# Softmax scores of two graph layers taken by streaming the edges past a one-column weight tile

## The reference

```python
# layer 1 ("attention")
z = feature @ W_out + b_out
e = gelu(z[src] @ attn_w[:d] + z[dst] @ attn_w[d:])
a = exp(e - segment_max(e, dst)[dst]); a = a / segment_sum(a, dst)[dst]
h = segment_sum(a[:, None] * z[src], dst) + feature @ res_W + res_b
# layer 2 ("relations")
att = sum(proj[src, etype] * tanh(proj[dst, etype] + efeat), axis=-1)
a = exp(att - segment_max(att, dst)[dst]); a = a / segment_sum(a, dst)[dst]
h_nb = segment_sum(nfeat[src] * a[:, None], dst)
```

## Time and profile before

| | |
|---|---|
| three runs | 4811.55, 4816.27, 4816.76 us; median 4816.27 |
| the profiled execution | 4814.14 us, of which 4812.4 us from its first to its last instruction (the span) |
| busy shares of the span | PE 85%, PEld 61%, DVE 67%, POOL 58%, ACT 41% |
| attention phase | from 1994 to about 2574 us |
| relation phase | from about 2577 to about 3775 us |
| granted clock of TensorE | 0.877 of full speed over the span; two levels occur, 2.4 GHz (1.00) and 1.2 GHz (0.50) |

### The profile page before, as it was taken

How to read it: one execution, slowest core, us unless ns; L and a number is a source line. 1 busy time by engine, 2 the same in 40 slices (tenths; PEclk the granted TensorE clock), 3 DMA queues, 4 the chain that set the end, 5 groups by cost and what they waited for, 6 DMA issues and landing times. The chain is left out here.

```text
span 4812.4 us, 78524 instructions
## 1 busy us (share of the span) xinstructions
PE 4094.3 (85%) x23907; PEld 2928.3 (61%) x24119; DVE 3210.3 (67%) x7115; ACT 1960.9 (41%) x3684; POOL 2811.1 (58%) x2859
## 2 busy tenths in 40 slices
PE   5989999799989999779986899898988677767776
PEld 1278888688877777578884455555555344444443
DVE  9967777666667888667776588888887433333332
ACT  0066666344445454224332155555555222222221
POOL 0066665667656666577753455554551377777777
PEclk9989999899989999755556899999998798899888
DMA  1089998799976676445543444444442222222221
GB/s 40 1 260 287 288 287 264 197 230 235 234 200 174 192 194 191 122 111 127 127 113 84 97 103 109 105 112 103 114 105 56 66 66 67 54 67 67 55 65 29
DMA packets 1127654, 649.03 MB, mean 135 GB/s; under 512 B 908912, under 2 KB 944313, under 8 KB 1127240
## 3 DMA queue, kind: packets, MB, share of 16 engines
q1 hardware_dynamic: 1039432, 555.85, 42.2%
q0 software_dynamic: 87808, 88.16, 9.2%
HBM read 384.70 MB, written 261.63 MB: 134 GB/s over the span
## 5 line engine op out<-in xcount | busy, mean ns | idle before, releaser
L2237 POOL DMA_INDIRECT r_got<-x_table,slot_idx x392 | 417.6, 1065 | 588.9 <-DVE r_masked L2470 280.7
L1089 POOL DMA_INDIRECT o_rows<-in_x_dram,dst_idx x392 | 370.7, 946 | 443.6 <-POOLq L348 241.7
L2552 POOL DMA_INDIRECT m_rows<-x_table,slot_idx x392 | 376.3, 960 | 223.6 <-issue 118.6
L2336 PE MATMUL r_source_t<-r_masked,rel_pair 64*128 64x512 f32 x980 | 501.3, 660 | 0.0
L2338 PE MATMUL r_own_t<-r_masked,rel_pair 64*128 64x512 f32 x980 | 501.2, 660 | 0.0
L2691 DVE TENSOR_TENSOR_SCAN m_both<-m_keep,m_both,m_rows_t 128x512 f32<-128x512 bf16 x97 | 124.1, 1279 | 553.1 <-PE m_rows_t L2614 553.1
L1541 POOL DMA_INDIRECT b_rows<-h_table,slot_idx x392 | 369.7, 943 | 206.9 <-issue 91.5
L1352 POOL DMA_INDIRECT a_got<-node_table,src_idx x392 | 375.5, 958 | 194.8 <-DVE a_conv L1488 57.3
L2560 POOL DMA_INDIRECT out_dram<-s_res,put_out x392 | 390.6, 996 | 137.8 <-issue 109.7
L2010 POOL DMA_INDIRECT t_got<-x_table,slot_idx x392 | 379.0, 967 | 144.8 <-issue 95.4
L2336 PEld LDWEIGHTS r_source_t<-r_masked,rel_pair 64*128 64x128 f32 x980 | 197.4, 211 | 239.0 <-issue 189.9
(11 more groups left out here) (401 smaller groups left out, 11670.1 us busy)
## 6 DMA issues: line engine op xcount, KB each, us to landing
x_table<-n_res SPq DMA_DIRECT2D x196, 256.0 KB
n_rows<-x_table SPq DMA_DIRECT2D x196, 256.0 KB
x_table<-s_res SPq DMA_DIRECT2D x294, 128.0 KB
node_table<-n_wide SPq DMA_DIRECT2D x98, 272.0 KB, 3.9
h_table<-n_conv SPq DMA_DIRECT2D x98, 256.0 KB
x_table<-s_res SPq DMA_DIRECT2D x98, 256.0 KB
r_feats<-in_edge_attr_dram SPq DMA_DIRECT2D x390, 64.0 KB
n_rows<-in_x_dram SPq DMA_DIRECT2D x97, 256.0 KB
```

The source lines that it names most:

```text
L1089: nc.gpsimd.indirect_dma_start(out=rows[:, n % 4, t, :], out_offset=None, in_=x, in_offset=bass.IndirectOffsetOnAxis(ap=dst_idx[:, n * TIL ...
L2237: nc.gpsimd.indirect_dma_start(out=got[:, n % RING, t, :], out_offset=None, in_=x2_table, in_offset=bass.IndirectOffsetOnAxis(ap=slot_idx[ ...
L2336: nc.tensor.matmul(source_t[:, :], rel_pair[0:D, k, :], masked[0:D, n % 2, k, :], start=(k == 0), stop=(k == PAIRS - 1), skip_group_check= ...
L2552: nc.gpsimd.indirect_dma_start(out=rows[:, n % 4, t, 0:D], out_offset=None, in_=x3_table, in_offset=bass.IndirectOffsetOnAxis(ap=slot_idx[ ...
```

## The change

`match` swaps the two operands. The weights are now a 128x128 tile that is zero but for one column: a window into a tile of 255 columns whose column 127 holds `score_col` (or ones). The window's offset puts this column at the tile's place in the chunk (0 to 27), and 128 edges are streamed past it. All 28 tiles of a chunk are summed into one 128x128 PSUM bank, whose first 28 rows then hold the chunk's scores in the softmax's layout; the other rows get zeros. In the attention phase one more matmul at a chunk's end adds the source part (`source_score` as weights against the identity), for which PE waits for DVE's `score_kept`. `add_scores` (DVE) and `turn_scores` (PE) are gone, ACT writes `score` into SBUF at once, and the wait for `shares_kept` moves from `turn_scores` to `turn_ends`. Each phase gets one or two more small instructions on DVE at its start that make the 255-column tile.

```diff
-            self.score_t = [pb(c, f"f_score_t{h}", [P, rows]) for h in range(score_banks)]
+            self.score_t = [pb(c, f"f_score_t{h}", [P, P]) for h in range(score_banks)]
-            self.score = self.small_t[0:rows, 384:384 + P]
-            self.kept_score = sb(c, "f_kept_score", [P, 2, rows])
+            self.score = sb(c, "f_score", [rows, P])
...
+        def slide(self, columns, n, t):
+            at = P - 1 - (self.row_of(n) * TILES + t)
+            return columns[:, at:at + P]
...
+        def keep(self, act, c, func, bias=None):
+            act.wait_ge(self.scored[c], self.scored.done(c))
+            if c >= 1:
+                act.wait_ge(self.belows[c - 1], self.belows.done(c - 1))
+            of = self.score_t[c % len(self.score_t)][0:self.rows, :]
...
+                nc.scalar.activation(self.score[:, :], of, func, bias=bias).then_inc(self.kept[c], 1)
...
-        def turn_scores(self, pe, c):
-            pe.wait_ge(self.kept[c], self.kept.done(c))
-            if c >= 1:
-                pe.wait_ge(self.shares_kept[c - 1], self.shares_kept.done(c - 1))
-            nc.tensor.transpose(self.score, self.kept_score[:, c % 2, :], ident[:, :]).then_inc(self.scores_turned[c], 1)
...
         def raise_rows(self, dve, c):
-            dve.wait_ge(self.scores_turned[c], self.scores_turned.done(c))
+            dve.wait_ge(self.kept[c], self.kept.done(c))
...
         def turn_ends(self, pe, c):
-                pe.wait_ge(self.total_entered[c - 1], self.total_entered.done(c - 1))
+                pe.wait_ge(self.shares_kept[c - 1], self.shares_kept.done(c - 1))
...
@@ attention_phase
                     def match(n):
                         pe.wait_ge(scanned[n], scanned.done(n))
-                        if n // CHUNK >= 2:
-                            pe.wait_ge(score_added[n // CHUNK - 2], score_added.done(n // CHUNK - 2))
+                        if n == 0:
+                            pe.wait_ge(cleared, 4)
+                        if n % CHUNK == 0 and n // CHUNK >= 2:
+                            pe.wait_ge(soft.kept[n // CHUNK - 2], soft.kept.done(n // CHUNK - 2))
                         for t in range(TILES):
-                            last = nc.tensor.matmul(soft.score_at(n, t), scan[:, n % SCANS, t * P:(t + 1) * P], score_col[:, :],
-                                                    start=True, stop=True, skip_group_check=True)
+                            nc.tensor.matmul(soft.bank_of(n)[:, :], soft.slide(score_cols, n, t), scan[:, n % SCANS, t * P:(t + 1) * P],
+                                             start=(n % CHUNK == 0 and t == 0), stop=False, skip_group_check=True)
                         if n % CHUNK == CHUNK - 1:
-                            last.then_inc(soft.scored[n // CHUNK], 1)
+                            k = n // CHUNK
+                            pe.wait_ge(score_kept[n], score_kept.done(n))
+                            nc.tensor.matmul(soft.bank_of(n)[0:soft.rows, :], source_score[:, k % 2].rearrange("p j t -> p (j t)"), ident[:, :],
+                                             start=False, stop=True, skip_group_check=True).then_inc(soft.scored[k], 1)
...
+                    nc.vector.memset(score_cols[:, :], 0.0).then_inc(cleared, 1)
+                    dve.wait_ge(cleared, 3)
+                    nc.vector.tensor_copy(score_cols[:, P - 1:P], score_col[:, :]).then_inc(cleared, 1)
...
@@ relation_phase
                         for t in range(TILES):
-                            last = nc.tensor.matmul(soft.score_at(n, t), pair[:, n % 2, t * P:(t + 1) * P], ones[:, 0:1],
-                                                    start=True, stop=True, skip_group_check=True)
+                            last = nc.tensor.matmul(soft.bank_of(n)[:, :], soft.slide(ones_cols, n, t), pair[:, n % 2, t * P:(t + 1) * P],
+                                                    start=(n % CH == 0 and t == 0), stop=(n % CH == CH - 1 and t == TILES - 1),
+                                                    skip_group_check=True)
...
+                    nc.vector.memset(ones_cols[:, :], 0.0).then_inc(cleared, 1)
+                    dve.wait_ge(cleared, 3)
+                    nc.vector.memset(ones_cols[:, P - 1:P], 1.0).then_inc(cleared, 1)
                     nc.vector.memset(scan[0:D, :, :], 0.0).then_inc(tops_cleared, 1)
```

More of the change, by code:

```diff
@@ L1765, in columns_of, with bank_of @@
             return slice(self.row_of(n) * TILES, self.row_of(n) * TILES + TILES)
[L1767 to L1772, removed]
+        def bank_of(self, n):
+            return self.score_t[n // self.chunk % len(self.score_t)]
+        def slide(self, columns, n, t):
+            at = P - 1 - (self.row_of(n) * TILES + t)
+            return columns[:, at:at + P]
         def load_first(self, sp):
@@ L1809, in raise_rows @@
                 dve.wait_ge(self.gaps[c - 1], self.gaps.done(c - 1))
-            nc.vector.tensor_tensor_scan(self.run(self.values()), self.run(self.low[:, c % 2, :]), self.run(self.score), LOW,
+            nc.vector.tensor_tensor_scan(self.run(self.values()), self.run(self.low[:, c % 2, :]), self.run(self.score[:, :]), LOW,
                                          ALU.add, ALU.max).then_inc(self.raised[c], 1)
@@ L1845, in raise_all @@
             dve.wait_ge(self.entered[c], self.entered.done(c))
-            nc.vector.tensor_tensor_scan(self.run(self.values()), self.run(self.low[:, c % 2, :]), self.run(self.score),
+            nc.vector.tensor_tensor_scan(self.run(self.values()), self.run(self.low[:, c % 2, :]), self.run(self.score[:, :]),
                                          self.entry(), ALU.add, ALU.max).then_inc(self.peaked[c], 1)
@@ L1852, in soften @@
                 dve.wait_ge(self.weighed[c - 1], self.weighed.done(c - 1))
-            nc.vector.tensor_tensor(self.below[:, :], self.score, self.values(), ALU.subtract).then_inc(self.belows[c], 1)
+            nc.vector.tensor_tensor(self.below[:, :], self.score[:, :], self.values(), ALU.subtract).then_inc(self.belows[c], 1)
             if c >= 1:
@@ L2088, in keep_chunk @@
                     def keep_chunk(eng, k):
-                        soft.keep(eng, k, ACT.Gelu, whole_score[:, k % 2, :], score_added, score_bias[:, 0:1])
+                        soft.keep(eng, k, ACT.Gelu, score_bias[0:soft.rows, 0:1])
                     def lift(b):
@@ L2154, in keep_shares @@
                         soft.keep_shares(eng, k, weighed, (k - 1) * CHUNK - 1)
[L2156 to L2161, removed]
-                                                source_score[:, k % 2].rearrange("p j t -> p (j t)"), ALU.add).then_inc(score_added[k], 1)
                     def invert(n):
@@ L2173, in _ @@
                                (scale, X + 3, BLOCKS), (powers, X + 2, BLOCKS), (keep_score, 1, BLOCKS),
-                               soft.after(2, add_scores, dve), soft.after(4, soft.raise_rows, dve), soft.after(5, soft.run_peaks, dve),
+                               soft.after(4, soft.raise_rows, dve), soft.after(5, soft.run_peaks, dve),
                                soft.after(6, soft.enter_peaks, dve), soft.after(6, soft.raise_all, dve), soft.after(6, soft.soften, dve),
@@ L2379, in _ @@
                                soft.after(6, soft.turn_ends, pe), soft.after(8, soft.turn_sums, pe), soft.after(9, turn_shares, pe),
[L2380 removed]
+                               soft.after(6, soft.turn_peaks, pe), soft.after(8, soft.turn_totals, pe),
                                (project, 2, BLOCKS))
@@ L2424, in keep_chunk @@
                     def keep_chunk(eng, k):
-                        soft.keep(eng, k, ACT.Copy, soft.scores_of(k), soft.scored)
+                        soft.keep(eng, k, ACT.Copy)
                     over_turns(soft.after(5, keep_chunk, act), (copy, 1, BLOCKS + X), (bend, 3, BLOCKS), (move, X + 1, BLOCKS), (move_own, X + 1, BLOCKS),
```

23 lines of the change are left out of this document (9 added, 14 removed).

## The result

The changed kernel takes 4787.41 us (median of three runs, 4784.41 to 4788.42) against 4816.27 us: a ratio of 0.9942 with a 95% interval of 0.9919 to 0.9964. That is 29 us less; 68 were forecast. The profiled execution's span is 4782.7 us against 4812.4, at a granted clock of 0.909 against 0.877.

What follows compares the result with a forecast made beforehand. POOL was taken to bound the attention phase, a ring across three engines the relation phase. -76 (relation clock) + 7 (`match`) + 1 (start) + 0 = -68 us gave 4748 us against the 4816.3 median; range for 8 in 10: 4712 to 4800.

Steps and rivals of the forecast that it cites:

- the price of the clock: Relation phase: each us of PE at 1.2 GHz costs 0.57 us, 0.50 in the first part.
- The attention phase is bound by POOL: Attention phase: gathers at 1.27 us each set 5.09 us a block; PE has 0.45 us to spare; change worth 0.
- The rival that it is PE-bound: Attention phase: PE bounds it and its clock rises; at best 70 us more gain, 4678 us; chance 7%.
- `match` in the ring, +7 us: Relation phase: `match` takes 0.07 us longer in each of 98 blocks, 7 us.
- Streams hide behind loads: `match`: 128 columns take as long as the weight load and still hide; 0.012 us more per matmul at 2.4 GHz.
- The ring through POOL: Relation phase: masks, gathers, POOL's multiply, `match`, `join`, next masks set a block, 9.75 us around.
- The clock answers to longer streams: Relation phase: with 128 columns per load in `match` the clock holds at 2.4 GHz; 95 us if no cold time is left.
- I keep a fifth: Relation phase: a fifth of the 95 us is not gained, because of chunk ends; 0.8 x 95 = 76 us gained.
- The sum: Whole kernel: -76 (relation clock) + 7 (`match`) + 1 (start) + 0 = -68 us.
- The last 90 us of the phase have no `match` and stay: End of the relation phase: its last 90 us, without `match`, do not change.
- only half of the cold time goes: Relation phase: falls of the clock move to other places in the block; -38 + 8 = -30, 4786 us; chance 9%.
- Start of the phase: Start of the relation phase: two small fills before the 9.02 us fill cost 1 us.

Runs made afterwards that it cites:

- e2: Kernel before with the change in the attention phase alone, relation phase as before: 4819.7 us, 0.9998.
- e4: Changed kernel with POOL's multiply moved ahead of the third gather of its turn, from behind the fourth: 4731.7 us, 0.9814.
- e7: Kernel before, scores as they were, with POOL's multiply moved ahead of the third gather of its turn: 4748.5 us, 0.9851.
- e3: Kernel before, all relation scores streaming 128 columns of ones instead of one past the same weights; transpose and copy kept: 4783.4 us, 0.9925.
- e9: Kernel before, 128 columns of ones streamed in relation scores only from period 21 on, in chunk middles (positions 1 to 4): 4820.6 us, 1.0024.
- e10: Kernel before, 128 columns of ones streamed in relation scores only from period 21 on, at chunk ends (positions 5, 6, 0): 4805.3 us, 0.9995.

## Why the prediction was off

**The failed step is the price of the clock, "so one us at 1.2 GHz costs 2.0 / 3.5 = 0.57 us", used for all of the 127 cold us behind the first part.** The price came from a block in the middle of a chunk, and there it is right in kind: place 2 gave 10.7 us for 23.9 cold us, 0.45. But two thirds of the cold time that went lay at chunk ends, where it gave 12.1 us for 54.6, 0.22. Of the 34 us that are missing behind the first part (53 forecast, 18.8 measured), the price accounts for some 22. One look at where in the chunks the falls are, and at one chunk end at 2.4 GHz (11.74 us a period, PE busy 9.57), would have shown it. I had noted chunk ends only as a place where falls might remain, not as one where they are cheap.

Point by point:
- The attention phase is bound by POOL: right. 497.9 us for 497.2, with PE down from 355 to 304 of 390 us, and e2 at 0.9998. The rival that it is PE-bound is out.
- `match` in the ring, +7 us: right in size. 2.91 us for 2.86 from `match` to the masks; the medians at 2.4 GHz grow by 0.06, 0.08 and 0.18 us at places 1, 3 and 4, and a chunk that is alike in both kernels (blocks 35 to 41) takes 75.57 us for 75.25. Streams hide behind loads: 128 columns for one add 0.11 us to the 1.05 us of `match`.
- The ring through POOL that was to set the middle blocks: right for this kernel, but only just. In e4 and e7 the wait before `match` is gone and places 1 to 3 still take 9.72 us, with the change and without it, so there the longer `match` costs nothing.
- The clock answers to longer streams: right, and e3 shows it alone. In the first part 0.84 became 1.00 and 47.8 cold us went for a gain of 16.5 us (0.35 each), where 22 us less some match time was forecast for all of it.
- "I keep a fifth": behind the first part 34.1 of 112.6 us stayed, 30%. And the 127 us were worked out from a rounded 0.93; the trace has 119.5 in that window. So 78.5 cold us went where 102 were counted on, which at 0.57 each is 13 of the 34 us missing: the second error, about half the size of the first.
- The sum: forecast for periods 21 to 97 some 58 us of clock less 5 of `match`; measured 18.8. By places: 10.7 (place 2) + 12.1 (places 5, 6, 0) - 4.0 (places 1, 3 and 4, which had no cold time and pay for `match`) = 18.8.
- "The last 90 us of the phase have no `match` and stay": they lost 4.5 us, by a fall that came in period 98 where before had none.
- The rival "only half of the cold time goes" named the right time, 4786 us, for a wrong reason: 126 of 171 cold us went. Its mechanism, falls that move, is real, though: e9 and e10 show it.
- Start of the phase: the transposes of block 2 come at 2606.9 us for 2606.6. Nothing to see of 1 us.

What stays open: why the clock falls at one place of a chunk and not at another, and so what decides between e9's pattern and e3's. The runs give the pattern only. Open too is why 3.4 cold us at place 6 cost nothing over the three periods, while 1.8 us more in `join` there cost 1.55. And that it is DVE which catches up behind a cold place 6 is read from the windows, not shown by a run of its own.

## What to carry to other kernels

Price a slow clock by the place where it is slow: list the stretches at 1.2 GHz, and for each ask whether PE ends last there; where the following block makes the lost time up, as behind place 6 here, the fall costs nothing. Look for small DVE instructions that take ten times their usual length: here 33 of them, beside POOL's multiply, were stretched by some 40 us in all, more than the 29 us of the whole change, and moving that one multiply in POOL's list gave some 56 us more. And before filling an engine's gaps with work to lift its clock, try to remove the wait that makes the gap.

## What the hardware showed that I had not expected

- A DVE instruction on 128x4 numbers takes 1.75 us beside POOL's 1.27 us multiply, and 0.16 us without it; 11 each of three kinds are held so, `s_masked` until POOL is done (`f_total` ends 0.28 us behind it), even where the DVE's record begins first (3147.52 against 3147.97). Once it was POOL that waited: at 3618.83 us of the changed kernel DVE's `r_mixed`, with two inputs in SBUF, begins with the multiply and takes its usual 0.69 us, and the multiply takes 1.82.
- The granted clock of the attention phase rose only to 0.69 to 0.74 when `match` streamed 128 columns, though PE was still busy 304 of 390 us, and it cost nothing to be low.
- Longer streams in some blocks made others fall: 112.6 cold us became 140.0 in e9.
